# Newton step of the eigenvalue merges: in-place fractions, one product for the discriminant, the absolute value on ScalarE, a weight product on GpSimd

## The reference

```
h = relu(layernorm(x));  x = x + L0(h, adj)      # input product, then 8 Euler steps on the graph
h = relu(layernorm(x));  x = x + L1(h, adj)      # this one needs eigh
h = relu(layernorm(x));  x = x + L2(h, adj)      # two batch norms
h = relu(layernorm(x));  x = x + L3(h, adj)      # graph layers, then short LSTMs

def L1(features, A):
    deg = sum(A, 0) + sum(A, 1) - diagonal(A);  L = diag(deg) - A
    _, U = eigh(rsqrt(deg)[:, None] * L * rsqrt(deg)[None, :])
    agg = einsum('mn,bnd->bmd', U.T, features)
    return einsum('nm,bmd->bnd', U, relu(agg @ W1 + b1) @ W2 + b2)
```

## Time and profile before

| | us |
|---|---|
| median of 3 runs | 4941.13 |
| lowest and highest | 4937.12, 4941.86 |
| profiled execution, its own time | 4943.4 |
| its span | 4941.6 |
| share of the span busy: PE, DVE, ACT, POOL | 77%, 66%, 22%, 8% |
| chain of work that ended last: PE, DVE, ACT | 48%, 44%, 3% |

### The profile page before, as it was taken

How to read it: one execution, slowest core, us unless ns; L and a number is a source line. 1 busy time by engine, 2 the same in 40 slices (tenths; PEclk the granted TensorE clock), 3 DMA queues, 4 the chain that set the end, 5 groups by cost and what they waited for, 6 DMA issues and landing times.

```text
span 4941.6 us, 71519 instructions
## 1 busy us (share of the span) xinstructions
PE 3781.6 (77%) x20546; PEld 1897.0 (38%) x20546; DVE 3279.5 (66%) x20976; ACT 1064.3 (22%) x4173; POOL 413.0 (8%) x1793
## 2 busy tenths in 40 slices
PE   4777777777778888888875667748965957599998
PEld 2333333333333333333354333425542623244433
DVE  5777777878888888888877898998822122202323
ACT  1111111222222222222201111101112122314542
POOL 0000000000000000000022221101100000000000
PEclk8999999999999999999956878879977978689998
DMA  2000000000000000000000000000000000000000
GB/s 86 2 1 1 2 1 1 2 1 1 2 1 1 1 2 1 1 1 1 1 1 1 1 1 1 1 0 1 1 0 0 0 17 0 0 0 0 0 0 34
DMA packets 3109, 21.11 MB, mean 4 GB/s; under 512 B 432, under 2 KB 560, under 8 KB 1072
## 3 DMA queue, kind: packets, MB, share of 16 engines
q1 hardware_dynamic: 2736, 16.85, 0.9%
HBM read 12.66 MB, written 4.19 MB: 3 GB/s over the span
## 4 chain that ended last, share of the span: by engine, by line
PE 48%; DVE 44%; ACT 3%; issue 3%; DMA 0%; POOL 0%; DVEq 0%; SPq 0%; POOLq 0%; ACTq 0%
PE ps L554 7%; PE ps L524 7%; PE ps L834 6%; DVE jq L1245 4%; PE ps L558 3%; PE ps L546 3%; DVE C L1424 2%; PE ps L841 2%; DVE tsc L1408 2%; DVE WG L1365 2%; DVE tsc L1418 2%; PE ps L530 2%; DVE tsc L1398 2%; DVE TMP L1360 2%; PE ps L806 1%
## 5 line engine op out<-in xcount | busy, mean ns | idle before, releaser
L546 PE MATMUL ps<-eye,same 128*128 128x512 f32 x2040 | 1200.4, 672 | 0.0
L563 PE MATMUL ps<-dots,ones 128*128 128x3 f32 x1020 | 199.2, 265 | 368.1 <-DVE dots L1245 367.5
L563 PEld LDWEIGHTS ps<-dots,ones 128*128 128x128 f32 x1020 | 161.4, 197 | 805.2 <-DVE dots L1245 803.8
L554 PEld LDWEIGHTS ps<-C 128*32 128x32 f32 x10200 | 255.2, 114 | 522.3 <-DVE C L1424 441.0
L554 PE MATMUL ps<-C 128*32 128x131 f32 (+39 forms) x10200 | 373.8, 277 | 76.1 <-DVE C L1424 21.3
L1079 ACT ACTIVATE sz<-C,tsc 128x4 f32<-128x4 f32 (+3 forms) x510 | 151.6, 297 | 1022.6 <-DVE tsc L1415 1022.6
L546 PEld LDWEIGHTS ps<-eye,same 128*128 128x128 f32 x2040 | 328.9, 203 | 0.0
L524 PE MATMUL ps<-C,LT 128*128 128x512 f32 x512 | 244.2, 622 | 91.9 <-ACT C L1071 91.9
L834 PE MATMUL ps<-C,V 128*128 128x512 f32 (+1 forms) x504 | 287.5, 727 | 8.5 <-issue 7.5
L884 POOL TENSOR_TENSOR xm<-C,WK 128x4 f32<-128x4 f32 (+3 forms) x510 | 101.0, 198 | 2275.0 <-DVE C L1424 1917.2
L1077 ACT ACTIVATE tsc<-tsc 128x1 f32<-128x1 f32 x510 | 103.4, 203 | 841.4 <-DVE tsc L1378 841.4
(11 more groups left out here) (468 smaller groups left out, 7127.4 us busy)
## 6 DMA issues: line engine op xcount, KB each, us to landing
out_x<-X SPq DMA_DIRECT2D x4, 1024.0 KB, 3.9
X<-in_x SPq DMA_DIRECT2D x2, 1280.0 KB, 20.5
X<-in_x SPq DMA_DIRECT2D x1, 1536.0 KB, 16.8
eye<-in_eye SPq DMA_DIRECT2D x1, 1026.0 KB, 9.4
WK<-in_adj SPq DMA_DIRECT2D x1, 1024.0 KB, 4.9
adjT<-in_adjT SPq DMA_DIRECT2D x1, 1024.0 KB, 7.0
WK<-in_below SPq DMA_DIRECT2D x1, 1024.0 KB, 11.2
V<-in_wih SPq DMA_DIRECT2D x1, 1024.0 KB, 4.9
```

The lines of the kernel that those rows point to most:

```text
L546: mm(ps[:, 7, 0:n], ident, eye[:, 0, 0:n], start=True, stop=True)
L554: mm(ps[q * QUAD:(q + 1) * QUAD, 0, 0:c + n], SI[:, b, 0, 2 * j:2 * j + 1].broadcast_to([P, QUAD]), AS[:, b, q, k * QUAD:P + n], start=(b ...
L563: mm(ps[:, 3, 0:3], ones[:], dots[:], start=True, stop=True).then_inc(S["dots_ps"], 1)
```

## The change

In a Newton step on DVE:

- a, c and b stay in `QF`: `QF[:, 1:3] -= UU` in place, and `c` becomes `-4 c` with the third sum in one instruction. The denominator `-4 c` and the numerator `b` then lie side by side in `QF[:, 2:4]`, so the copy into `ND` goes.
- a squared and `-4 c b` are one product over `128x8`, then one sum, where there were two products and a fused sum.
- `|a|` is taken by ACT (`absa`, after `a_ready`) ahead of the root, in each of the 72 steps; DVE waits for `abs_ready` beside `sqrt_ready`.
- The comparison into `X8` moves to the middle of the coefficients. The first instruction is now waited for by the second.

In the head, DVE loses two small instructions on `L8` and the grid product on `LEf`, and gains a small one (`gap4`); the start point is computed in one instruction from `t1` and `hg`. POOL takes over in step 0, between `K8` and `Q6`: the product on `LEf` (now with minus four times the gap), then three small ones for `L8`. DVE waits for `le_ready` before it reads `LEf`.

In the end of levels 0 to 6, the two products with PSUM rows become one of twice the length.

The diff, cut to its core:

```diff
@@ GpSimd, step 0 of a level, after K8
+                        g_.tensor_tensor(grid(LEf, lv), grid(LEf, lv), col_grid(cn["gap4"], lv), ALU.mult).then_inc(S["le_ready"], 1)
+                        product(L8[:, 0:4], cn["t1"], cn["hg"])
+                        product(L8[:, 4:8], L8[:, 0:4], cn["hg"], ALU.add)
+                        scaled(L8[:, 4:8], L8[:, 4:8], -1.0, ALU.mult)
@@ ScalarE, each step
+                    act.wait_ge(S["a_ready"], lv * NEWTON + it + 1)
+                    fn(small("absa"), QF[:, 1, :], ACT.Abs).then_inc(S["abs_ready"], 1)
@@ VectorE, head
-                step(tt(L8[:, 0:4], cn["t1"], cn["hg"], ALU.mult))
-                step(stt(L8[:, 4:8], L8[:, 0:4], -1.0, cn["hg"], ALU.mult, ALU.subtract))
-                step(stt(MU[0], gap, 0.25, L8[:, 0:4], ALU.mult, ALU.add))
-                step(tt(grid(LEf, lv), grid(LEf, lv), col_grid(gap, lv), ALU.mult))
+                step(ts_(cn["gap4"], gap, -4.0, None, ALU.mult))
+                step(stt(MU[0], cn["t1"], 0.5, cn["hg"], ALU.add, ALU.mult))
@@ VectorE, each step
-                    stt(QF, twice(fsum[:, 0:4], 4), 1.0, Q6[:, 0:4, :], ALU.add, ALU.mult).then_inc(S["qf_ready"], 1)
+                    step(stt(QF, twice(fsum[:, 0:4], 4), 1.0, Q6[:, 0:4, :], ALU.add, ALU.mult))
                     step(tt(pair(UU), twice(fpf), Q6[:, 3:5, :], ALU.mult))
-                    step(tt(pair(CM), QF[:, 1:3, :], pair(UU), ALU.subtract))
-                    step(tt(CM[:, 4:8], CM[:, 4:8], fsum[:, 8:12], ALU.add))
-                    step(tt(PR[:, 0:4], a, a, ALU.mult))
-                    step(tt(PR[:, 4:8], c, b, ALU.mult))
-                    step(stt(cn["disc"], PR[:, 4:8], -4.0, PR[:, 0:4], ALU.mult, ALU.add))
+                    step(ts_(pair(X8), QF[:, 0:3:2, :], 0.0, None, ALU.is_gt))
+                    tt(QF[:, 1:3, :], QF[:, 1:3, :], pair(UU), ALU.subtract).then_inc(S["a_ready"], 1)
+                    dve.wait_ge(S["a_ready"], i + 1)
+                    step(stt(QF[:, 2, :], QF[:, 2, :], -4.0, fsum[:, 8:12], ALU.mult, ALU.add))
+                    step(tt(pair(PR), QF[:, 1:3, :], QF[:, 1:4:2, :], ALU.mult))
+                    step(tt(cn["disc"], PR[:, 0:4], PR[:, 4:8], ALU.add))
                     ts_(cn["disc"], cn["disc"], 1e-34, None, ALU.max).then_inc(S["disc_ready"], 1)
-                    step(ts_(ND[:, 0:4], c, -4.0, None, ALU.mult))
-                    v.tensor_copy(ND[:, 4:8], b).then_inc(S["qf_ready"], 1)
-                    step(ts_(pair(X8), QF[:, 0:3:2, :], 0.0, None, ALU.is_gt))
                     v.copy_predicated(L8, X8.bitcast(U32), PM8).then_inc(S["lo_ready"], 1)
-                    step(stt(cn["t2"], a, -1.0, a, ALU.mult, ALU.max))
                     step(stt(pair(MK), twice(a), 0.0, pair(zeros_ones), ALU.is_gt, ALU.subtract))
                     dve.wait_ge(S["sqrt_ready"], lv * (NEWTON + 1) + it + 1)
-                    step(tt(cn["t1"], cn["t2"], cn["root"], ALU.add))
-                    put(pair(ND), pair(MK), twice(cn["t1"]))
+                    dve.wait_ge(S["abs_ready"], i + 1)
+                    step(tt(cn["t1"], cn["absa"], cn["root"], ALU.add))
+                    put(QF[:, 2:4, :], pair(MK), twice(cn["t1"]))
@@ VectorE, end of a level
-                    for c in range(2):
-                        half = TTf[:, c * nb:(c + 1) * nb]
-                        go(tt(grid(half, lv), grid(VVf, lv), row_grid(ps[:, c, :], lv), ALU.mult))
-                        ch.wait()
+                    if lv < TOP:
+                        step(tt(TTf[:, 0:2 * nb].rearrange("p (c t) -> p c t", c=2), VVf[:, 0:nb].unsqueeze(1).broadcast_to([P, 2, nb]),
+                                ps[:, 0:2, 0:n4], ALU.mult))
```

More of the change, by code:

```diff
@@ L313, in build @@
                  "es_in", "es_ps", "qt_zero", "tables_ready", "rhs_ready", "row_ready", "z2_sb", "fl_in", "fl_ps", "f2_ready", "sign_in", "sign_out", "idg_ready",
-                 "mu_ready", "pq_ready", "qf_ready", "pm_ready", "lo_ready", "br_ready", "disc_ready", "sqrt_ready", "v_ready", "vx_ready", "vt_ps", "vt_sb",
+                 "mu_ready", "pq_ready", "qf_ready", "a_ready", "abs_ready", "le_ready", "pm_ready", "lo_ready", "br_ready", "disc_ready", "sqrt_ready", "v_ready", "vx_ready", "vt_ps", "vt_sb",
                  "qn_ps", "qn_sb", "u_ps", "z_ready", "gram_ps", "gram_sb", "y_ps", "y_sb", "z2_ps", "x_upd", "vtr_ps", "vtr_sb",
@@ L361, in build @@
         QF = jqf[:, 24:40].rearrange("p (s c) -> p s c", s=4)
-        PR, UU, ND, MK, CM, X8, PM8, L8, M8, K8, DND = (jqf[:, 40 + 8 * n:48 + 8 * n] for n in range(11))
+        PR, UU, MK, CM, X8, PM8, L8, M8, K8, DND = (jqf[:, 40 + 8 * n:48 + 8 * n] for n in range(10))
         F2, ZZ8, TZ, ZR8, FR8, S8 = (SOf[:, 8 * n:8 * n + 8] for n in range(6))
@@ L366, in build @@
         CN = ("D", "kept", "gone", "t1", "mx", "mx2", "Ds", "ub", "zn", "has", "gap0", "hg", "f", "neg", "right", "lo", "disc",
-              "root", "den", "t2", "sk", "sa", "sb", "rden")
+              "root", "den", "t2", "sk", "sa", "sb", "rden", "gap4", "absa")
         def small(name):
@@ L1645, in merge @@
                         step(tt(t1, t0, big_of(RRf, lv), ALU.mult))
+                        if it == 0:
+                            dve.wait_ge(S["le_ready"], lv + 1)
                         step(tt(t2, t1, big_of(LEf, lv), ALU.mult))
@@ L1671, in merge @@
+                    tt(QF[:, 1:3, :], QF[:, 1:3, :], pair(UU), ALU.subtract).then_inc(S["a_ready"], 1)
+                    dve.wait_ge(S["a_ready"], i + 1)
+                    a = QF[:, 1, :]
+                    step(stt(QF[:, 2, :], QF[:, 2, :], -4.0, fsum[:, 8:12], ALU.mult, ALU.add))
+                    step(tt(pair(PR), QF[:, 1:3, :], QF[:, 1:4:2, :], ALU.mult))
+                    step(tt(cn["disc"], PR[:, 0:4], PR[:, 4:8], ALU.add))
                     ts_(cn["disc"], cn["disc"], 1e-34, None, ALU.max).then_inc(S["disc_ready"], 1)
-                    step(ts_(ND[:, 0:4], c, -4.0, None, ALU.mult))
@@ L1681, in merge @@
-                    dve.wait_ge(S["qf_ready"], 2 * i + 2)
-                    put(pair(ND), pair(MK), twice(cn["t1"]))
-                    step(v.reciprocal(cn["rden"], ND[:, 0:4]))
-                    step(tt(cn["t1"], ND[:, 4:8], cn["rden"], ALU.mult))
+                    dve.wait_ge(S["abs_ready"], i + 1)
+                    step(tt(cn["t1"], cn["absa"], cn["root"], ALU.add))
+                    put(QF[:, 2:4, :], pair(MK), twice(cn["t1"]))
+                    step(v.reciprocal(cn["rden"], QF[:, 2, :]))
@@ L1685, in merge @@
+                    step(tt(cn["t1"], QF[:, 3, :], cn["rden"], ALU.mult))
                     step(stt(cn["t1"], cn["t1"], 2.0, mu, ALU.mult, ALU.add))
@@ L1735, in merge @@
                     dve.wait_ge(S["fl_ps"], lv + 1)
-                    for c in range(2):
-                        half = TTf[:, c * nb:(c + 1) * nb]
-                        go(tt(grid(half, lv), grid(VVf, lv), row_grid(ps[:, c, :], lv), ALU.mult))
+                    if lv < TOP:
+                        step(tt(TTf[:, 0:2 * nb].rearrange("p (c t) -> p c t", c=2), VVf[:, 0:nb].unsqueeze(1).broadcast_to([P, 2, nb]),
+                                ps[:, 0:2, 0:n4], ALU.mult))
+                    else:
+                        for c in range(2):
+                            go(tt(grid(TTf[:, c * nb:(c + 1) * nb], lv), grid(VVf, lv), row_grid(ps[:, c, :], lv), ALU.mult))
                         ch.wait()
-                        if c == 1 or w == 2 * P:
-                            v_n = 8 if w < 2 * P else 4
                     m = v.tensor_reduce(F2, TTf[:, 0:2 * nb].rearrange("p (c t) -> p c t", t=w), AX.X, ALU.add)
```

5 lines of the change are left out of this document (removed).

## The result

| | before | after |
|---|---|---|
| median, us | 4941.13 (five runs, 4934.58 to 4952.09) | 4913.13 (five runs, 4910.9 to 4916.65) |
| ratio of the times | | 0.9944, 95% interval 0.993 to 0.9959 |
| profiled execution, its own time | 4943.4 | 4910.9 |
| its span | 4941.6 | 4909.1 |

A forecast was written before the change was run, and what follows sets the result against it. ACT, taking roots and evictions in turn, joins DVE's Newton chain to PE's Euler tiles; DVE is last in 32 of 72 steps. -13.9 + 0.7 - 6.5 + 2.5 - 1.3 = -18.5 us gives 4922.7 us, range 4912 to 4932.

The forecast's parts named there:

- Which steps count: Merges: DVE is last in 32 of 72 Newton steps, and only these keep the gain of 0.435 us each.
- The runs: Gapless PE work on Euler units, ending where DVE waits; levels 0, 6, 8 should stay 47.1, 85.8, 244.9 us.
- Rival A: Merges: no run of Euler units binds and all 72 steps keep their gain; 4905 us, chance 0.06.
- Part 1: DVE's small instructions in a Newton step: 1.90 us instead of 2.34; 32 x 0.435 = -13.9 us.
- rival D: Merges: added waits eat the saved instructions, so the 32 steps gain nothing; 4937 us, chance 0.05.
- Part 2: Absolute value on ACT: free where DVE is last, elsewhere 0.12 us in each of six levels; +0.7 us.
- Part 3: Head of a level: DVE sheds small instructions and the grid product, a gain in six levels; -6.5 us.
- part 5: End of a level: one product of twice the length instead of two, in seven levels; -1.3 us.
- Part 4: GpSimd in step 0: four more products delay DVE in levels 0, 2 and 3, hidden elsewhere; +2.5 us.
- rival B: GpSimd's work costs more than it covers, its product stretching DVE's reciprocal in levels 6 to 8; 4931 us, chance 0.13.

The follow-up runs named there:

- the kernel before with the new table: The kernel before with only another table of Euler unit counts for the 72 slots, found by replaying the changed kernel's durations; 4887.4 us, ratio 0.9883.

## Why the prediction was right, point by point

The time of 4913.13 lies only 1.1 us inside the range of 4912 to 4932. What the prediction had right is the stage that it worked out, 18.5 against 19.0. Part of even that is luck: levels 0 to 4 and 7 came out 1.3 short of their sums, levels 5, 6 and 8 1.9 over, and the reasons below (clock, collisions) are not the prediction's.

**Which steps count: right.** This was the term that decided, 32 steps and not 72, and the level table bears it out with no level off by more than 0.7. The runs kept their length, and DVE's waits for roots grew by 14.0 (at least 10 forecast). Rival A is out by the runs, and is what the kernels without units do.

**Part 1, a step: right.** 1.90 to 1.91 in all steps where DVE is last, 1.41 + 0.20 + 0.29. The gain is 0.43 to 0.44, so rival D is out. What the prediction did not do is ask what else the shifted chain meets. In level 5 additions to X on POOL held up four of DVE's small instructions by 1.0 each before (among them the one of the earlier trace rows). After it two held a small one by 1.1 each, one held a grid product, 1.37 instead of 0.42, and one ran beside a reciprocal and held only the product behind it, by 0.2:

```profile
2877.86 1.26 POOL L973 TENSOR_TENSOR X<-X,C 128x512 f32<-128x512 f32 x1
2877.89 1.24 DVE L1685 TENSOR_TENSOR sm<-jq,sm 128x4 f32<-128x4 f32 x1
...
2882.25 1.51 POOL L973 TENSOR_TENSOR X<-X,C 128x512 f32<-128x512 f32 x1 [3.13 <-ACT C L1075]
2882.68 1.37 DVE L1649 TENSOR_TENSOR H<-H 128x256 f32<-128x256 f32 x1
```

That is 3.4 instead of 4.1 in all, which covers level 5's 0.7.

**Part 2, the absolute value: right where it was asked, incomplete.** Where a root is late, L1141 and L1143 start 0.10 apart (2965.84 and 2965.94 in level 6), near the 0.12 taken. Putting it back on DVE did not win these 0.7 but lost 3.4: 0.04 a step, since two instructions fit behind the discriminant for free and a third not quite, and the most of it, 3.0, in two groups of matmuls at a lower clock.

**Part 3, the head: right.** The heads of levels 1 and 4 to 8 end 0.41, 0.53, 0.67, 1.11, 1.65 and 2.65 earlier than before, 7.0 in all. Of that 0.5 is part 5's (0.19 in levels 6 and 7, 0.12 in level 8, where two products no longer wait for each other), so the head itself gave the 6.5. Between the last roots of levels 7 and 8 the change gave 2.91: 2.69 up to the first root (2.4 forecast), 0.2 in the run.

**Part 4, GpSimd: right in size, by another path.** The cost was 1.03 + 0.94 + 0.54 = 2.5, as forecast. The rows foreseen, one wait of 1.5 to 2 us at the first coefficients, are two: 1.22, 0.93 and 0.81 for the mask `LEf` in levels 0, 1 and 2, then 1.21, 1.18 and 1.11. No reciprocal grew, so rival B is out.

**Part 5, the end of a level: right in size, mostly lost.** From the first product to the sum behind it takes 0.19 less in each of the seven levels, as forecast (1.44 and 1.26 in level 6, for example), 1.3 in all. But at the start of levels 1 to 5 a product of POOL (L908, 1.04 to 1.27) begins at the same event as before, and DVE's first instruction of the level ends only after it. Level 1, before and then after:

```profile
2557.19 0.41 DVE L1549 TENSOR_TENSOR SO<-SO,TMP 128x8 f32<-128x8 f32 x1
```

```profile
2547.22 1.04 POOL L908 TENSOR_TENSOR C<-C,same 128x512 f32<-128x512 f32 x1 [14.31 <-DVE C L1733]
...
2547.69 0.60 DVE L1555 TENSOR_TENSOR SO<-SO,TMP 128x8 f32<-128x8 f32 x1
```

It starts 0.19 earlier and is held 0.19 longer, and so it is in levels 2 to 4 too (0.15 in level 5). In a level without this neighbour it takes 0.17. So 0.9 of the 1.3 never came out. The products stand behind a level's last root, so in the level table their gain would belong to the level after; with it left out up to level 5, levels 0 to 3 come within 0.05 of their sums. The prediction had looked for this collision between DVE and POOL only where work was moved, not where DVE became earlier.

**A wait that the prediction missed.** The longest wait of DVE for POOL, 4.5, is not at the start of a level but in level 7, after step 2. POOL's list has the additions of a slot ahead of the next step's `Q6`. The trace after:

```profile
3139.83 0.60 ACT L1075 ACTIVATE C<-ps 128x512 f32<-128x512 f32 x1 [4.59 <-PE ps L530]
3140.50 1.26 POOL L973 TENSOR_TENSOR X<-X,C 128x512 f32<-128x512 f32 x1 [3.71 <-ACT C L1075]
...
3142.28 0.20 POOL L948 TENSOR_TENSOR jq<-jq 128x4 f32<-128x4 f32 x1
...
3142.59 0.17 DVE L1667 SCALAR_TENSOR_TENSOR jq<-SO,jq 128x16 f32<-128x16 f32 x1 [4.47 <-POOL jq L948]
```

and before, the same place:

```profile
3169.07 0.17 DVE L1661 SCALAR_TENSOR_TENSOR jq<-SO,jq 128x16 f32<-128x16 f32 x1 [2.66 <-issue]
```

DVE waits for POOL, POOL for ACT, ACT for PE: a second place where the Newton chain hangs on the units, besides the root. It took 1.8 us more of what DVE had gained. It did no harm to the sum, since level 7 was counted at no steps anyway. What it is behind in the earlier trace rows is hidden: the view of before puts 2.66 of it down to "issue".

**The level of the time: off by 9.5, outside the merges.** The sum took the rest of the kernel as fixed. 3.5 of it came behind the merges, in both pairs of executions, 2.6 of them within 80 us of the last root. Windows of the trace before (stretch, us, busy time and count of PE, PEld, DVE, ACT and POOL, granted clock, DMA), the first 56 us from the last root and the next 80:

```profile
3583.40:3639.40 56.00, 35.24 (x144) 25.27 (x144) 14.58 (x23) 6.03 (x6) 2.26 (x2) 0.79 0.00 0
3639.40:3719.40 80.00, 48.29 (x209) 35.11 (x208) 20.93 (x41) 9.30 (x12) 0.00 (x0) 0.83 0.00 0
```

and of the trace after:

```profile
3554.40:3610.40 56.00, 33.88 (x144) 23.85 (x144) 15.88 (x26) 6.02 (x6) 2.26 (x2) 0.82 0.00 0
3610.40:3690.40 80.00, 49.03 (x211) 35.43 (x212) 20.21 (x39) 9.29 (x12) 0.00 (x0) 0.86 0.00 0
```

The granted clock is 0.79 and 0.83 before, 0.82 and 0.86 after. The same pair of matmuls, some 53 us behind the last root, is at the lower level (1.2 GHz) in the trace before:

```profile
3636.59 0.63 PE L693 MATMUL ps<-C 128*128 128x128 f32 x2
```

and at the higher (2.4 GHz) after:

```profile
3607.30 0.39 PE L693 MATMUL ps<-C 128*128 128x128 f32 x2
```

That it is not the code of that stage is shown by the kernel before with the new table (1354.6 behind the merges): it has the code of the kernel before in that stage, and the time of the kernel after. (The kernel before without units took 1354.5, but it also leaves out a wait at the start of this stage.) The changed kernel with the head on DVE took 1356.0. Which property of the merges decides what clock is granted behind them stays open.

The remaining 5.5 of the 28.0 are left for the stage ahead, if what lies behind the merges is the same in every execution. Chance is part of what is seen there: fourteen profiled executions of it, all with the same code, took from 2458.9 to 2479.7 us, and a set of twelve runs of the kernel before had a median 4.5 below another. But chance alone does not cover it: over all runs on record the two kernels differ by 27.3 (24.8 to 29.7), some 5 more than the 22.5 that the traces place, and no run of one kernel reaches those of the other. The cause of these 5 us stays open. So of the 9.6 by which the forecast of 4922.7 was too high, 0.5 is the merges', 3.5 lies behind them and goes with the granted clock, and 5.6 is unexplained.

## What to carry to other kernels

Before a saved instruction is counted, ask in which steps its engine is the last one: here the in-order list of ACT bound a chain of small instructions to long runs of units of PE, and the steps at which a run ends give nothing back. Compare kernels by stages between two events that both have; a median over the whole time mixed 19 us of effect with 9 of other things. Give a difference of 1 us or so to an edit only after looking at the matmuls beside it: in five of the experiments, levels that differed by 0.4 to 1.6 us owed most of it to a group of matmuls at another granted clock. And where waits grow after an engine was made faster, the next gain lies in the placing of the other work: a table of counts, found by replaying measured durations, was worth 55 us where eliminating instructions was worth 19.
